# A graph transformer on one core: half of the attention's stacking copies issued by ScalarE in every group

## The reference

```
# block A, 8 heads of 32
nx = layernorm(x) * g1 + b1
q, k, v = nx @ wq + bq, nx @ wk + bk, nx @ wv + bv
scores = q k^T / sqrt(32) + (0.1 * adj * adj where adj > 0, else -inf)
x1 = x + softmax(scores) v @ wo + bo
x2 = x1 + gelu(layernorm(x1) * g2 + b2 @ w1 + ...) @ w2 + ...      # hidden 1024
# layers C0 and C1, one head of 128
q, k = x @ Wq^T + bq, x @ Wk^T + bk
attn = softmax(q k^T / sqrt(128), masked by adj)
x = layernorm(x + attn x Wc^T) * g + b
```

## Time and profile before

| what | value |
|---|---|
| median of 3 runs | 2104.08 us (2099.52 to 2104.42) |
| profiled execution | 2106.19 us, span 2103.9 us |
| PE, DVE, ACT, POOL busy | 1877.8, 1699.8, 1563.6, 1019.8 us |
| chain that ended last | PE 61%, ACT 14%, DVE 10%, POOL 9%, issue 4% |
| mean granted clock of PE | 0.969 |

### The profile page before, as it was taken

How to read it: one execution, slowest core, us unless ns; L and a number is a source line. 1 busy time by engine, 2 the same in 40 slices (tenths; PEclk the granted TensorE clock), 3 DMA queues, 4 the chain that set the end, 5 groups by cost and what they waited for, 6 DMA issues and landing times.

```text
span 2103.9 us, 44316 instructions
## 1 busy us (share of the span) xinstructions
PE 1877.8 (89%) x15704; PEld 1351.8 (64%) x15704; DVE 1699.8 (81%) x3398; ACT 1563.6 (74%) x2996; POOL 1019.8 (48%) x1304
## 2 busy tenths in 40 slices
PE   4778899999999999999999999999999999999884
PEld 2545567666666666666666676666666666666662
DVE  3766788888888888888888888888888888888653
ACT  1466677778877777888777778877777788777651
POOL 2012335555544555555445555554555555445575
PEclk9698899999999999999999999999999999999997
DMA  6223344433344443333444443344444334444211
GB/s 151 66 46 81 91 101 101 103 85 82 86 110 101 111 101 95 84 84 91 101 111 111 101 86 82 85 101 101 111 103 104 82 82 87 108 101 86 66 36 41
DMA packets 441610, 192.46 MB, mean 91 GB/s; under 512 B 347760, under 2 KB 416368, under 8 KB 441392
## 3 DMA queue, kind: packets, MB, share of 16 engines
q1 hardware_dynamic: 440368, 188.04, 38.1%
q0 software_dynamic: 544, 0.80, 0.3%
q10 hardware_dynamic: 480, 0.79, 0.2%
HBM read 38.55 MB, written 16.78 MB: 26 GB/s over the span
## 4 chain that ended last, share of the span: by engine, by line
PE 61%; ACT 14%; DVE 10%; POOL 9%; issue 4%; DMA 1%; SPq 1%; DVEq 0%; POOLq 0%; ACTq 0%
PE ps L327 17%; PE ps L329 16%; PE ps L328 16%; PE ps L1296 6%; POOL area L543 4%; PE ps L1361 3%; DVE st L746 2%; DVE area L759 2%; ACT L683 2%; ACT cs L704 2%; POOL hid_l L334 2%; DVE area L899 2%; ACT L704 2%; POOL rs L538 2%; POOL ve L536 2%
## 5 line engine op out<-in xcount | busy, mean ns | idle before, releaser
L662 ACT ACTIVATE area<-area,nmax 128x128 f32<-128x128 f32 x1024 | 312.6, 390 | 17.0 <-DVE nmax L874 16.3
L536 POOL TENSOR_TENSOR ve<-mv,eps_cols 128x4 f32<-128x4 f32 x128 | 62.4, 487 | 479.2 <-DVE mv L751 479.0
L334 POOL TENSOR_TENSOR hid_l<-area,hid_h 128x512 f16<-128x512 f32 x128 | 156.5, 1223 | 284.7 <-ACT hid_h L686 284.7
L327 PE MATMUL ps<-w_h,hid_h 128*128 128x256 f16 x1024 | 279.2, 273 | 13.6 <-POOL hid_l L334 12.5
L329 PE MATMUL ps<-w_h,hid_l 128*128 128x256 f16 x1024 | 279.0, 272 | 0.0
L328 PE MATMUL ps<-w_l,hid_h 128*128 128x256 f16 x1024 | 279.0, 272 | 0.0
L683 ACT ACTIVATE area<-ps,b_col 128x512 f32<-128x512 f32 x256 | 176.1, 688 | 44.7 <-PE ps L329 38.0
L327 PE MATMUL ps<-rot_h,w_h 128*128 128x512 f16 x512 | 198.7, 388 | 8.6 <-ACT area L683 5.4
L328 PE MATMUL ps<-rot_l,w_h 128*128 128x512 f16 x512 | 197.5, 386 | 0.0
L329 PE MATMUL ps<-rot_h,w_l 128*128 128x512 f16 x512 | 197.5, 386 | 0.0
L543 POOL TENSOR_TENSOR area<-area,cwb_row 128x256 f32<-128x256 f32 x128 | 89.9, 732 | 198.5 <-ACT area L712 198.5
(11 more groups left out here) (200 smaller groups left out, 5911.3 us busy)
## 6 DMA issues: line engine op xcount, KB each, us to landing
qkS<-qk SPq DMA_DIRECT2D x378, 128.0 KB, 2.3
xin<-in_x SPq DMA_DIRECT2D x32, 512.0 KB, 4.6
adj_in<-in_adj SPq DMA_DIRECT2D x64, 256.0 KB, 2.8
out<-x SPq DMA_DIRECT2D x30, 512.0 KB, 2.8
area<-in_L_gnn_w SPq DMA_DIRECT2D x1, 1024.0 KB, 7.2
area<-in_L_gnn_w SPq DMA_DIRECT2D x2, 512.0 KB, 10.3
rot_h<-sA_h SPq DMA_TRANSPOSE x64, 2.8
rot_l<-sA_l SPq DMA_TRANSPOSE x64, 2.7
```

The source lines that it names most:

```text
L327: pe.matmul(dst, lh, rh, start=start, stop=False, **kw)
L334: eng.tensor_tensor(hid_l[:, c % RING, :], hidden[:, c % 2, :], hid_h[:, c % RING, :], ALU.subtract).then_inc(done, 1)
L662: last = act.activation(sc[:, b % 2, h], sc[:, b % 2, h], ACT.Exp, bias=nmax[:, b, h:h + 1])
```

## The change

ACT's list gets a step `Q.stk+0` between `A.PT3-1` and `C0.ex-3`. It issues the six copies of head places 2 and 3 for every group, with the waits that SP's step has, each with its increment. SP's step, in its old place, issues only head places 0 and 1. The special case of the first group ahead of `Q.v1` goes away.

```diff
-          "A.exp3-1", "Q.k1+0", "A.PT3-1", "C0.ex-3", "C0.xW-3", "A.oT-1", "C0.PT-3", "M.up7-2",
+          "A.exp3-1", "Q.k1+0", "A.PT3-1", "Q.stk+0", "C0.ex-3", "C0.xW-3", "A.oT-1", "C0.PT-3", "M.up7-2",
...
                         for slot, parts in enumerate((slice(0, 3, 2), slice(0, 4, 3), slice(1, 3, 1))):
-                            for j in range(2 if g == (0, 0) else 4):
+                            for j in range(2):
                                 sp.dma_start(qkS[32 * slot:32 * slot + 32, :, j],
                                              qk16[32 * j:32 * j + 32, parts]).then_inc(stk, 16)
...
                 elif step == "Q.v1":
-
-                    for i in range(4):
-                        act.wait_ge(d_qk[i], 1)
-                    for slot, parts in enumerate((slice(0, 3, 2), slice(0, 4, 3), slice(1, 3, 1))):
-                        for j in range(2, 4):
-                            act.dma_start(qkS[32 * slot:32 * slot + 32, :, j],
-                                          qk16[32 * j:32 * j + 32, parts]).then_inc(stk, 16)
                     act.wait_ge(ld_wo, 16)
...
+                    elif what == "stk":
+                        need_apart(act, t_S, g, B, 0)
+                        for i in range(4):
+                            need_apart(act, a_qk[i], g, 1, 1)
+                            need_apart(act, d_qk[i], g, 1, 1)
+                        for slot, parts in enumerate((slice(0, 3, 2), slice(0, 4, 3), slice(1, 3, 1))):
+                            for j in range(2, 4):
+                                act.dma_start(qkS[32 * slot:32 * slot + 32, :, j],
+                                              qk16[32 * j:32 * j + 32, parts]).then_inc(stk, 16)
```

## The result

The changed kernel took 2236.52 us (median of 4 runs, 2234.63 to 2238.79), the kernel before beside it 2103.32 us: the ratio is 1.0634, 95% interval 1.0618 to 1.065. It is slower by 133 us where 92 had been forecast: outside the forecast's own range (2183 to 2205), and inside the stated one, which had been drawn wide enough to hold two rivals. The profiled execution took 2235.82 us with a span of 2233.5, so 129.6 us more span than before (2103.9). Lines move by four behind the new step: L672 of before is L676 of after, L704 is L708, L712 is L716, L1352 is L1356, and L668, the probabilities' copy, is L672.

The account below looks back on a forecast made before the run. The prediction took the chain through PE and ACT's A.oT as the bound, with stacking not late. SP's relief 0, A.oT 3.15 us later in 29 iterations, 91.4 us, gave 2196 us; own range 2183 to 2205, 8-in-10 range 2182 to 2250.

Parts of the forecast that it names:

- the stated one: The 8-in-10 range for the whole time, drawn to reach over rivals A and B: 2182 to 2250 us.
- What bounds the kernel: Chain through PE, DVE, A.oT and M.up7 on ACT; 0.27 us room ahead of A.oT; stacking not late in regular iterations.
- The issues hold ACT: ACT's step ahead of C0.ex: activations cannot overtake the issues; C0.ex starts 0.05 us behind the last, 3.42 us later.
- the one instance at 42.54: First group, kernel before: activation behind ACT's six issues started 0.05 us after their end, though free four microseconds earlier.
- The start of the issues: ACT behind A.PT3: first issue at 1058.40, 0.11 us behind DVE's last key part (1058.29), beside the running copy.
- rival A: Issues wait for A.PT3's copy to end, then increments, starting at 1059.85: 2241 us; chance 0.18.
- The length: ACT's six issues take 4.06 us, as in the first group beside SP's issues; SP alone takes 3.86.
- Rival C: ACT's issues and SP's transposes lock each other out, 2.5 us more per iteration: 2268 us; chance 0.05.
- A.oT's delay: A.oT on ACT comes 3.15 us later per iteration: C0.ex's 3.42 less 0.27 of room.
- The clock: PE's gap ahead of L1352 is about 2.6 us, nearer to a harmless 2.4 than to 3.4; clock stays at 1.00.
- Rival B: PE's gap lowers its clock, 1.4 us of PE work lost each time, 40 us in all: 2236 us; chance 0.08.
- Sum: Iterations 3 to 31: 29 x 3.15 = 91.4 us, giving 2196 us, 4.3% slower; iteration 63.6 us.

Follow-up runs that it names:

- the relief alone: Kernel before with the copies of head places 2 and 3 left out for all groups but the first, ACT issuing nothing there: 2100.67 us, ratio 1.0001.
- three issues: Changed kernel with three of the twelve copies on ACT and nine on SP, first group as before: 2137.16 us, ratio 1.0162.
- the run with one wait: Changed kernel with one of ACT's nine waits left, that for DVE's low part of the last keys: 2205.76 us, ratio 1.0504.

## Why the prediction came out as it did

**What bounds the kernel.** Right as to the path: the stacking was not late, A.oT is on the chain, and the relief alone gave a ratio of 1.0001. Wrong as to the room: "That 0.27 us is all the room there is" took A.oT's wait for the whole of it, and 0.55 us were measured, with three issues and with six.

**The issues hold ACT.** Right, from the one instance at 42.54: C0.ex started 0.05 us behind the last issue again, and the waits count 29 such stalls. The Trainium skill ("Advanced Engine Details and Errata", "Sequencer and Instruction Queues") has engine instructions pushed into a queue of their own, and the traces agree for the activation ahead of the issues: in the run with one wait it overlaps them by 0.8 us. Its other half, that further engine instructions can be read and queued while a control instruction is worked on, would have let C0.ex overtake, as the prediction read it, if a DMA issue counted as such an instruction; C0.ex never did.

**The start of the issues.** Mis-sized: 1058.40 in the trace of before, 0.23 us behind the copy's start, was foretold, and 0.73 was measured. I took only the wait for the last key part as binding and let the eight other waits and increments be done before; they are taken after the copy has been handed over, and cost 0.5 us (nine in SP's trace: 0.66). It was neither my start nor rival A's, which had the increments behind the copy's end (1.68). With one wait the foretold 0.11 us behind DVE appeared.

**The length.** 4.26 us, 4.06 foretold; the 0.2 lie in the last two issues, beside SP's transposes. Rival C's lock-out, with 2.5 us more, did not happen: 0.4 is all that the crowding costs.

**A.oT's delay.** 3.57 us, 3.15 foretold: 0.5 from the start and 0.2 from the length make 3.85, less 0.28 for the room that had been missed. Some 0.15 of it lies ahead of C0.xW, which starts 1.70 us behind C0.ex in the earlier trace rows and 1.55 in the changed kernel. The other 0.13 lies behind it: A.oT, when it waits for nothing, starts 0.10 us before C0.xW's end (1061.80 against 1060.90 + 1.00), and not at it.

**The clock.** This is the step that failed most. Rival B's mechanism came with the forecast's own. I held the gap for 2.6 us (by the prediction's own rows it is 1065.2 - 1062.49 = 2.7) and nearer to one of 2.4 that had left the clock alone than to one of 3.4, and gave it 0.08. (The first row has the clock of that gap only; in the trace it stays at 1.00 for 15 us behind it.) The gap was 3.16 us, and behind 27 of the 29 gaps the clock fell. Behind a gap of 3.13 us, at 282.61, it stayed at 1.00, and that iteration took 63.99 us, 0.9 less than the others. Even the gap of 2.4, in the run with one wait, brought it down in most of them. The price, 1.4 us of work, was a little low: 0.79 over 8 us is 1.7. Of that 0.9 reached the chain, since M.down7 had to wait for POOL anyway. Rival B's 2236 us is the measured 2236.52 by luck: it had 0.4 us too little for the hold in each iteration and 0.5 too much for the clock.

**Sum.** 3.57 + 0.91 = 4.48 us, where the median iteration grew from 60.44 to 64.90, 4.46. 29 times 4.48 is 129.9, against 129.6 us of span; that it fits so closely is partly luck. The clock stayed up behind two of the 29 gaps; against that A.oT came 0.8 us late already in the first iterations, where nothing had been foretold, and a few iterations grew by 5.2 to 5.6.

## What to carry to other kernels

A DMA issue is work for the engine that makes it, though no busy time counts it: some 0.64 us each in these kernels, in line with its compute. Before issues move to another engine, look whether the queue they leave was late at all, and put them where the new engine waits and where their transfers don't meet one that somebody waits for. Where an added wait opens a gap on PE, price the clock behind the gap too, and don't take one gap that passed for a bound.

## What was not expected

With one wait on ACT, three gaps of PE of 2.42, 2.37 and 2.37 us in neighbouring iterations, with the same work around them, ended in a granted clock of 0.79, 1.00 and 0.79 over the next 8 us. In the run with the step behind M.up7 (nine waits), the clock fell in one iteration behind a gap of 1.73 us that left it at 1.00 in the iterations beside it; the changed kernel and four other runs have one such fall each behind that gap (1.73 or 2.0 us), the kernel before none in 28. What decides in such a case stayed open.

Giving PE 12 useless matmuls for each group made the changed kernel 23 us faster.

A shorter wait made a kernel slower (2114.51 to 2127.59 us), by sending copies out beside a transpose that somebody waited for and that was late already. The median landing of that transpose moved from 2.7 to 2.8 us only; the total of PE's waits for it, from 11.2 to 24.7 us, is where it can be seen.
